# Layer norms of a two-layer perceiver block: GpSimd makes the offset, ScalarE scales the rows, and one norm stands for two

## The reference

```python
def _layernorm(x, axis=-1, eps=1e-05):
    m = jnp.mean(x, axis=axis, keepdims=True)
    v = jnp.var(x, axis=axis, keepdims=True)
    return (x - m) / jnp.sqrt(v + eps)

x = x + cross_attention(ctx, _layernorm(x))        # 16 heads, 4096 keys
x = x + top64_attention(_layernorm(x))             # 16 heads, 256 keys, only the 64 largest scores
x = x + switch_ffn(_layernorm(x))                  # 8 experts, capacity 128
x = x + context_attention(_layernorm(x), ctx)      # 1 head, 4096 keys
x = x + state_space(_layernorm(x))                 # both directions, see below
x = x + tile_ffn(_layernorm(x))                    # 8 tiles, one chosen per row
```

## Time and profile before

| | |
|---|---|
| median of 3 runs | 1524.51 us (1522.3 to 1524.8) |
| the profiled execution | 1535.18 us, its span 1533.7 us |
| PE busy, share of the span | 1304.3 us, 85% |
| PEld | 805.7 us, 53% |
| DVE | 1259.5 us, 82%, 3917 instructions |
| ACT | 973.0 us, 63%, 1505 instructions |
| POOL | 418.7 us, 27%, 316 instructions |
| mean granted PE clock, share of full | 0.909 |

### The profile page before, as it was taken

One profiled execution on the slowest core, in us unless ns is written; L12 is line 12 of the kernel. 1 busy time (PEld: TensorE's weight loads), 2 busy tenths in 40 slices (PEclk: granted clock), 3 DMA queues, 4 the chain that ended last, 5 costly groups with the idle time before them and its releaser, 6 DMA issues. The chain is left out here.

```text
span 1533.7 us, 31701 instructions
## 1 busy us (share of the span) xinstructions
PE 1304.3 (85%) x11784; PEld 805.7 (53%) x11784; DVE 1259.5 (82%) x3917; ACT 973.0 (63%) x1505; POOL 418.7 (27%) x316
## 2 busy tenths in 40 slices
PE   7999899998999988999958597678879789567746
PEld 4555566655665655666634484366347446323313
DVE  1355059999999998999999999998997787878983
ACT  6777778888786876878833353266677578434330
POOL 4110012232322213222222321222343343422450
PEclk9999999999998998999979799879979979678767
DMA  7878320333213320330005122104466356223320
GB/s 158 216 189 266 57 32 30 53 57 57 29 29 57 57 32 28 57 53 14 33 23 176 42 78 89 55 29 136 137 170 180 102 139 180 79 59 111 93 74 7
DMA packets 96856, 132.69 MB, mean 87 GB/s; under 512 B 20192, under 2 KB 80872, under 8 KB 93744
## 3 DMA queue, kind: packets, MB, share of 16 engines
q1 hardware_dynamic: 96688, 130.50, 33.6%
HBM read 124.95 MB, written 5.51 MB: 85 GB/s over the span
## 5 line engine op out<-in xcount | busy, mean ns | idle before, releaser
L1434 ACT ACTIVATE attn_arena<-ps 128x1024 f32<-128x1024 f32 x512 | 497.5, 1025 | 142.4 <-PE ps L456 139.6
L2066 DVE MATCH_REPLACE8 attn_late<-attn_shared,attn_late 128x256 f32<-128x256 f32 x1024 | 411.6, 410 | 0.0
L2063 DVE MAX8 attn_shared<-attn_late 128x8 f32<-128x256 f32 x1024 | 381.3, 415 | 11.9 <-ACT attn_late L1460 10.7
L456 PE MATMUL ps<-attn_arena 32*128 32x256 f32 x4096 | 343.0, 407 | 7.8 <-ACT attn_arena L1434 3.2
L470 PE MATMUL ps<-attn_arena 128*32 128x256 f32 x4096 | 279.0, 389 | 6.5 <-ACT attn_early L1442 3.0
L456 PEld LDWEIGHTS ps<-attn_arena 32*128 32x128 f32 x4096 | 231.4, 188 | 92.8 <-issue 65.4
L1297 POOL TENSOR_SCALAR attn_late<-attn_late 128x512 f32<-128x512 f32 x64 | 95.7, 1495 | 595.1 <-DVE attn_late L2066 595.1
L470 PEld LDWEIGHTS ps<-attn_arena 128*32 128x32 f32 x4096 | 109.2, 110 | 138.8 <-issue 63.1
L739 PE MATMUL ps<-attn_arena,attn_q 128*128 128x512 f32 x256 | 134.4, 660 | 15.0 <-DMA attn_arena<-ctxT 15.0
L1310 POOL TENSOR_TENSOR attn_late<-attn_late 128x1024 f32<-128x1024 f32 x48 | 113.2, 2362 | 121.5 <-DVE ps L1889 121.5
L761 PE MATMUL ps<-attn_arena 128*128 128x256 f32 x512 | 128.1, 396 | 0.0
(11 more groups left out here) (249 smaller groups left out, 1622.7 us busy)
## 6 DMA issues: line engine op xcount, KB each, us to landing
attn_arena<-ctxT SPq DMA_DIRECT2D x124, 256.0 KB, 4.7
attn_arena<-ctx SPq DMA_DIRECT2D x32, 512.0 KB, 4.2
attn_late<-rows SPq DMA_DIRECT2D x256, 64.0 KB, 2.3
attn_arena<-ctxV SPq DMA_DIRECT2D x15, 1024.0 KB, 13.0
attn_late<-maskT SPq DMA_DIRECT2D x20, 512.0 KB, 6.6
attn_late<-wide SPq DMA_DIRECT2D x64, 128.0 KB, 2.7
attn_early<-wide SPq DMA_DIRECT2D x64, 128.0 KB, 3.3
attn_arena<-maskT SPq DMA_DIRECT2D x12, 512.0 KB, 11.9
```

Source lines behind the costliest of these rows:

```text
L456: mm = pe.matmul(ps[:, first + j - 2 * i, u * S:(u + 1) * S], kx[n % 2][rows, k0:k0 + P], qpad[rows, n % GROUPS, b * S:(b + 1) * S], start ...
L1434: act.activation(probs[m % 2][:, 2 * i:2 * i + 2], ps[:, first:first + 2, :], ACT.Exp, scale=1.0 / 16.0).then_inc(exp_done, 1)
L2063: dve.max(top[:, t, turn], s[:, i, t] if turn == 0 else work[:, i, t]).then_inc(picked, 1)
L2066: dve.match_replace(work[:, i, t], top[:, t, turn], s[:, i, t] if turn == 0 else work[:, i, t], LOW).then_inc(picked, 1)
```

## The change

For the norms `out`, `place` and `fx` DVE stops after `ve`; POOL makes `rstd` and the offset -mean * rstd (`nmean`), and ACT writes the rows as Identity(x * rstd + nmean) in a slot of its own. For the state space block one set of statistics is left. With v the first variance, the second norm has factor rstd * spread, with spread = (v * rstd^2 + EPS)^-0.5, and the residual x + n has factor rstd + 1; POOL works both out in ten small instructions and ACT writes `xs` and `X` from them. `x0` and `xn` stay as they were. POOL waits for `normed` (ACT done with the last factors) before it writes `rstd` again; DVE waits for the last `rstd_ready` before it writes new statistics.

```diff
+def norm_order():
+    first = {("x0", b): FIRST_P + (b + 1) * 2 for b in range(B)}
+    first |= {("xn", b): H * b - LEAD + 2 for b in range(B)}
+    first |= {(name, b): DUE[name][b][0] + 1 for name in ("out", "place") for b in range(B)}
+    first |= {("ssm", b): SSM_P[b] - 6 for b in range(B)}
+    first |= {("fx", b): FFN_P[b] + 9 for b in range(B)}
+    return {name: i for i, name in enumerate(sorted(first, key=first.get))}
...
-            def root(k):
+            def root(k, alone=False):
                 pool.wait_ge(var_ready, k + 1)
-                pool.tensor_tensor(rstd[:], ve[:], mhalf[:], ALU.pow).then_inc(rstd_ready, 1)
+                pool.wait_ge(normed, scaled[0])
+                power = pool.tensor_tensor(rstd[:], ve[:], mhalf[:], ALU.pow)
+                if alone:
+                    power.then_inc(rstd_ready, 1)
+                    return
+                scaled[0] += 1
+                step(power)
+                step(pool.tensor_tensor(nmean[:], mv[:, :, 0], rstd[:], ALU.mult))
+                pool.tensor_scalar(nmean[:], nmean[:], -1.0, None, ALU.mult).then_inc(rstd_ready, 1)
+
+            def roots_twice(k):
+                pool.wait_ge(var_ready, k + 1)
+                pool.wait_ge(normed, scaled[0])
+                scaled[0] += 1
+                step(pool.tensor_tensor(rstd[:], ve[:], mhalf[:], ALU.pow))
+                step(pool.tensor_tensor(spread[:], rstd[:], rstd[:], ALU.mult))
+                step(pool.tensor_tensor(spread[:], spread[:], mv[:, :, 1], ALU.mult))
+                step(pool.tensor_scalar(spread[:], spread[:], EPS, None, ALU.add))
+                step(pool.tensor_tensor(spread[:], spread[:], mhalf[:], ALU.pow))
+                step(pool.tensor_tensor(twice[:], rstd[:], spread[:], ALU.mult))
+                step(pool.tensor_tensor(nmean[:], mv[:, :, 0], rstd[:], ALU.mult))
+                step(pool.tensor_scalar(nmean[:], nmean[:], -1.0, None, ALU.mult))
+                step(pool.tensor_tensor(ntwice[:], nmean[:], spread[:], ALU.mult))
+                pool.tensor_scalar(rstd[:], rstd[:], 1.0, None, ALU.add).then_inc(rstd_ready, 1)
...
                 for b in batches(-6, p):
-                    root(roots[0])
-                    root(roots[0] + 1)
-                    roots[0] += 2
-                    pool.wait_ge(xs_ready, b + 1)
+                    roots_twice(roots[0])
+                    roots[0] += 1
+                    pool.wait_ge(xs_ready, T * (b + 1))
...
+            def scale_rows(name, b, rows, ready):
+                act.wait_ge(rstd_ready, norm_index[name, b] + 1)
+                act.activation(rows[:, 0], X[:, b * T], ACT.Identity, scale=rstd[:, 0:1], bias=nmean[:, 0:1]).then_inc(ready, 1)
+                act.activation(rows[:, 1], X[:, b * T + 1], ACT.Identity, scale=rstd[:, 1:2], bias=nmean[:, 1:2]).then_inc(ready, 1)
+                act.wait_ge(ready, T * (b + 1))
+                act.sem_inc(normed, 1)
+
+            def scale_twice(b):
+                name = "ssm"
+                act.wait_ge(rstd_ready, norm_index[name, b] + 1)
+                for t in range(T):
+                    act.activation(xs[:, t], X[:, b * T + t], ACT.Identity, scale=twice[:, t:t + 1], bias=ntwice[:, t:t + 1]).then_inc(xs_ready, 1)
+                for t in range(T):
+                    x = X[:, b * T + t]
+                    act.activation(x, x, ACT.Identity, scale=rstd[:, t:t + 1], bias=nmean[:, t:t + 1]).then_inc(x_summed, 1)
+                act.wait_ge(x_summed, T * (b + 1))
+                act.sem_inc(normed, 1)
...
             def late_duties(p, slot):
...
+                for b in due_after("out", p - 1):
+                    if b < B - 1 and slot == 0:
+                        scale_rows("out", b, xm, xm_ready)
+                for b in due_after("out", p):
+                    if b == B - 1 and slot == 1:
+                        scale_rows("out", b, xm, xm_ready)
+                for b in due_after("place", p):
+                    if slot == (3 if b == B - 1 else 2):
+                        scale_rows("place", b, xc, xc_ready)
+                if slot == 2:
+                    for b in batches(-6, p):
+                        scale_twice(b)
+                if slot == 0:
+                    for b in ffn_batches(10, p):
+                        scale_rows("fx", b, xm, fx_ready)
...
-            def normalise(k, x, out):
+            def normalise(k, x, out=None):
+                if k > B:
+                    dve.wait_ge(rstd_ready, k)
                 for t in range(T):
                     step(dve.bn_stats(stats[:, t], x[:, t]))
                     step(dve.bn_aggr(mv[:, t], stats[:, t]))
                 dve.tensor_scalar(ve[:], mv[:, :, 1], EPS, None, ALU.add).then_inc(var_ready, 1)
+                if out is None:
+                    return
...
             def ssm_norms(b):
-                x = X[:, b * T:(b + 1) * T]
-                step(normalise(norms[0], x, xs))
-                norms[0] += 1
-                dve.tensor_tensor(x, x, xs, ALU.add).then_inc(dve_step, 1)
-                count[0] += 1
-                normalise(norms[0], xs, xs).then_inc(xs_ready, 1)
+                normalise(norms[0], X[:, b * T:(b + 1) * T])
                 norms[0] += 1
...
                     for b in batches(9, p):
+                        dve.wait_ge(x_summed, T * (b + 1))
                         add(b, "sout")
```

More of the change, by code:

```diff
@@ L289, in attention @@
         ve = sb("ve", [P, T])
-        rstd = sb("rstd", [P, T])
+        rstd, nmean = sb("rstd", [P, T]), sb("nmean", [P, T])
+        twice, ntwice, spread = sb("twice", [P, T]), sb("ntwice", [P, T]), sb("spread", [P, T])
         mhalf = sb("mhalf", [P, T])
@@ L399, in attention @@
         ssm_loaded, a_exp, a_ready, ssm_zeroed, ssm_consts = sem("ssm_loaded"), sem("a_exp"), sem("a_ready"), sem("ssm_zeroed"), sem("ssm_consts")
-        xs_ready, xs2_ready, cv_ready, u_ready, xcd_ready = sem("xs_ready"), sem("xs2_ready"), sem("cv_ready"), sem("u_ready"), sem("xcd_ready")
+        xs_ready, x_summed, xs2_ready, cv_ready, u_ready, xcd_ready = sem("xs_ready"), sem("x_summed"), sem("xs2_ready"), sem("cv_ready"), sem("u_ready"), sem("xcd_ready")
         rows_stored, bc_loaded, act_step, l_ready, dt_ready = sem("rows_stored"), [sem(f"bc_loaded{i}") for i in range(BC_HELD)], sem("act_step"), sem("l_ready"), sem("dt_ready")
@@ L420, in attention @@
         PICKS = 4 * (TOPK // 8)
-        misc, branch = {}, {}
+        misc, branch, norm_index = {}, {}, norm_order()
         block = ctx.enter_context(nc.Block())
@@ L957, in _ @@
                     for b in due("xm", p, slot):
-                        pe.wait_ge(xm_ready, b + 1)
+                        pe.wait_ge(xm_ready, T * (b + 1))
                         turn_rows("xm", b, xm)
@@ L966, in _ @@
                     for b in due("xc", p, slot):
-                        pe.wait_ge(xc_ready, b + 1)
+                        pe.wait_ge(xc_ready, T * (b + 1))
                         turn_rows("xc", b, xc)
@@ L1318, in _ @@
             pool.memset(kx[0][:, FIRST_KT * P:], 0.0).then_inc(kx_zeroed, 1)
-            root(0)
+            root(0, alone=True)
             pool.wait_ge(x0_ready, 1)
@@ L1346, in _ @@
                 if p - FIRST_P + 1 in INTRO:
-                    root(INTRO[p - FIRST_P + 1])
+                    root(INTRO[p - FIRST_P + 1], alone=True)
                 if 0 <= p - 1 < B * H:
@@ L1364, in _ @@
                 if ending and d == 2:
-                    root(roots[0])
+                    root(roots[0], alone=True)
                     roots[0] += 1
@@ L1967, in between @@
                         add(b, "out")
-                        normalise(norms[0], X[:, b * T:(b + 1) * T], xm).then_inc(xm_ready, 1)
+                        normalise(norms[0], X[:, b * T:(b + 1) * T])
                         norms[0] += 1
@@ L1977, in between @@
                             add_expert(b)
-                            normalise(norms[0], X[:, b * T:(b + 1) * T], xc).then_inc(xc_ready, 1)
+                            normalise(norms[0], X[:, b * T:(b + 1) * T])
                             norms[0] += 1
@@ L2034, in between @@
                     for b in batches(9, p):
+                        dve.wait_ge(x_summed, T * (b + 1))
                         add(b, "sout")
                     for b in ffn_batches(9, p):
-                        normalise(norms[0], X[:, b * T:(b + 1) * T], xm).then_inc(fx_ready, 1)
+                        normalise(norms[0], X[:, b * T:(b + 1) * T])
                         norms[0] += 1
```

6 lines of the change are left out of this document (3 added, 3 removed).

## The result

Five runs of the changed kernel took 1507.67 to 1515.83 us, median 1512.98, against 1524.8 us for the kernel before (1522.3 to 1526.79): ratio 0.9914 (95% interval 0.9889 to 0.994). A second set gave 1511.88 us and 0.9900 (0.9879 to 0.9922). The change saves 12 to 15 us; 17.3 were forecast.

The account below looks back on a forecast made before the run. DVE was taken to bound the attention steps, with mixed bounds in the scan steps. The terms -15.3 + 1.6 + 2.8 + 1.7 - 5.4 - 3.3 + 0.6 sum to -17.3 us: 1507.2 us from 1524.5, range 1488 to 1516.

Parts of the forecast that it names:

- rival 2: Attention steps: PE takes part of the gain, about 5 to 10 us lost, 1512 to 1517 us; chance 0.14 together with rival 4.
- Steps 20 to 58: Six plain norms and one state space norm relieve DVE and PE can follow: -15.3 us, ends 0 and -17.
- 3 (all): Slots where ACT waits for POOL: PE and ACT's stream becomes the bound, +16.8 us, 1541 us; chance 0.05.
- Steps 66 to 73: Forecast for steps 66 to 72: DVE's relief absorbed, POOL's L1310 starts later behind ACT: +1.6 us, ends -8.7 and +3.
- step 74: Same chain through POOL, SP's keys and PE; L1310 later, delay comes through at once: +2.8 us, ends -5.4 and +5.
- Steps 81 to 83: fx of batch 0 delays make_log, +1.7 us; batch 3's state space norm gets its rows sooner, -5.4 us.
- the row that it had allowed to shrink: DVE's 3.38 us row at 1340.03, beside POOL's L1310; shrinking by 2.35 us would make step 83's gain -7.8 us.
- The rest: fx of batches 1 and 2, in steps where DVE runs through with short waits: -3.3 us, end 0.
- The tail: Last fx, serial: DVE's 0.82 us become 0.55 us on POOL and 0.91 us on ACT: +0.6 us.
- Relief in full: Whole kernel: all of DVE's norm relief counts, 39.3 us, giving 1485.2 us; chance 0.23 for it or most of it.
- rival 4: New ACT lines: Identity loads a function table each time, about 1517 us; chance 0.14 together with rival 2.

Follow-up runs that it names:

- before_weigh: Kernel before, with POOL's first weigh_states of state space norm steps moved right behind the two roots, ahead of the norm_w and norm_b products; ratio 1.0011.
- ssm_only: Changed kernel with norms out, place and fx back on DVE, so only the state space norm is changed; ratio 0.9970 to the kernel before.
- after_keys: Changed kernel with SP's context key loads one slot earlier, ahead of the B and C loads; ratio 0.9883 to the kernel before.
- after_store: Changed kernel with SP's stores of dt and du ahead of the first B and C load of their step; ratio 0.9924 to the kernel before.
- after_both: Changed kernel with both SP moves, key loads one slot earlier and stores ahead of the first B and C load; ratio 0.9861 to the kernel before.
- after_fx: Changed kernel with ACT writing the fx rows at the end of slot 1, behind make_log, instead of in slot 0; ratio 0.9890 to the kernel before.
- plain_only: Changed kernel with the state space block's two norms back on DVE, so only out, place and fx are changed; ratio 0.9971 to the kernel before.
- before_both: Kernel before with both SP moves, key loads one slot earlier and stores ahead of the first B and C load; ratio 0.9983.
- before_keys: Kernel before with SP's context key loads one slot earlier, ahead of the B and C loads; ratio 1.0008.
- after_weigh: Changed kernel with POOL's first weigh_states of state space norm steps ahead of its wait for ACT's rows and the norm products; ratio 0.9857 to the kernel before.
- after_all: Changed kernel with all four moves: SP's keys and stores, POOL's weigh_states, ACT's fx rows; 1499.89 us, ratio 0.9824 to the kernel before.

## Why the prediction was right, and where not

From the median of 1524.5 us the forecast was 1507.2 us, with 1500 to 1511 as its own range. Measured are 1512.98 and 1511.88 us, 1 to 2 us outside that range and inside the wide one (1488 to 1516). By the number alone rival 2 (1512 to 1517) fits about as well; what decides is where the time went, stretch by stretch. There the terms miss by 0.2 to 1.9 us, with both signs, so that the sum (-15.0 against -17.3) is no further off is in part luck.

**Steps 20 to 58: -15.3 forecast, -13.4 measured.** The mechanism is as written. Step 58 after the change:

```profile
966.15 0.17 DVE L1805 TENSOR_SCALAR attn_ve<-attn_mv 128x2 f32<-128x2 f32 x1
966.23 1.21 DVE L1895 TENSOR_REDUCE attn_mx<-attn_arena 128x1 f32<-128x1024 f32 x1
```

DVE goes on at once, where 5.44 us lay before. Each plain norm moved the following selects by 1.7 us against before_weigh (1.65 forecast), and step 58 by 4.2 to 4.8, by the profile compared (5.44; 5.5 in ssm_only). Between steps 46 and 54 up to 0.9 us are given back; what takes them is not shown. Less than 2 of the 15.3 us are missing. So PE's room was enough for nearly all of it, and rivals 2 (5 to 10 us lost) and 3 (all) are out.

**Steps 66 to 73: +1.6 forecast, -0.2 measured; step 74: +2.8 forecast, +2.1 measured.** That the 5.44 us of two norms would be absorbed, and that step 74 would even lose, was the step that made the forecast, and it held: at scans 4 and 5 the profile after had gained 5.7 us more than at scan 0 (-26.2 us against -20.5), and at scan 10 it was back at -20.7; at step 74, from scan 20 to 24, it went from -26.4 to -18.0. At step 66 the delay was smaller than forecast: L1344 starts 9.4 us after `ve` began, 9.2 before. Step 74 after the change, in order:

```profile
1187.40 0.17 DVE L1805 TENSOR_SCALAR attn_ve<-attn_mv 128x2 f32<-128x2 f32 x1
1188.61 1.22 DVE L1953 TENSOR_TENSOR ps<-attn_late,attn_early 128x1024 f32<-128x1024 f32 x1
1188.71 1.17 POOL L1201 TENSOR_TENSOR attn_spread<-attn_spread,attn_mv 128x2 f32<-128x2 f32 x1
...
1192.21 0.22 POOL L1208 TENSOR_SCALAR attn_rstd<-attn_rstd 128x2 f32<-128x2 f32 x1
1194.79 1.09 ACT L1643 ACTIVATE attn_early<-X,attn_ntwice,attn_twice 128x256 f32<-128x256 f32 x2
1195.97 1.27 POOL L1436 TENSOR_TENSOR attn_early<-attn_early,attn_arena 128x512 f32<-128x512 f32 x1 [3.54 <-ACT attn_early L1643]
1198.87 2.79 POOL L1344 TENSOR_TENSOR attn_late<-attn_late 128x1024 f32<-128x1024 f32 x1
1201.68 1.71 SPq L1112 DMA_DIRECT2D attn_late<-rows  x4
1203.44 1.85 SPq L1092 DMA_DIRECT2D attn_arena<-ctxT  x4
...
1207.22 0.43 SPq L1116 DMA_DIRECT2D wide<-attn_early  x1
...
1207.57 5.70 PE L749 MATMUL ps<-attn_arena,attn_q 128*128 128x512 f32 x8 [4.77 <-DMA attn_arena<-ctxT]
...
1213.39 1.86 SPq L1132 DMA_DIRECT2D attn_early<-wide  x4
...
1216.84 1.22 DVE L1895 TENSOR_REDUCE attn_mx<-attn_arena 128x1 f32<-128x1024 f32 x1 [6.11 <-ACT attn_arena L1563]
...
1218.22 1.23 DVE L1953 TENSOR_TENSOR ps<-attn_late,attn_early 128x1024 f32<-128x1024 f32 x1 [0.16 <-DMA attn_early<-wide]
```

POOL has its ten small ones done at 1192.43, stands 3.54 us for ACT, which is in `make_log` until 1194.4, and starts L1344 11.5 us after `ve` began (9.2 us before). Everything behind it on SP starts from there. What the forecast got wrong is what hangs on it. It named the keys alone, and said that PE's wait for them would grow; it is 4.77 us here and 4.95 at step 66, not longer than the 5.11 and 5.00 of the earlier trace rows. The wait that grew is DVE's, 6.11 us now at L1895 and 1.21 us at the same place before:

```profile
1234.87 1.22 DVE L1826 TENSOR_REDUCE attn_mx<-attn_arena 128x1 f32<-128x1024 f32 x1 [1.21 <-ACT attn_arena L1530]
```

after_keys and after_store, each without effect, and after_both with 6 to 8 us show that the stores are a second chain of the same length; they stand in the kernel before too, and the forecast left them out.

**Steps 81 to 83: +1.7 and -5.4 forecast, -3.7 together; -2.2 measured.** The stretch from scan 30 to 44 shows -3.9, but 1.7 of that is `fx` of batch 1, which lies between scans 43 and 44. The remaining -2.2 us hide two larger errors that partly cancel: `fx` of batch 0 cost 4.7 us instead of 1.7, and the state space norm gave 6.7 instead of 5.4; the last 0.2 us are in a wait for PE. That the sum is near is luck. Step 82:

```profile
1292.23 1.24 POOL L1193 TENSOR_SCALAR attn_nmean<-attn_nmean 128x2 f32<-128x2 f32 x1
...
1293.50 0.60 ACT L1634 ACTIVATE attn_xm<-X,attn_nmean,attn_rstd 128x256 f32<-128x256 f32 x1 [7.05 <-POOL attn_nmean L1193]
...
1296.32 0.45 ACT L1599 ACTIVATE attn_early<-ps,attn_arena 128x256 f32<-128x256 f32 x1
...
1308.28 0.69 DVE L1848 TENSOR_TENSOR X<-X,ps 128x512 f32<-128x512 f32 x1 [6.37 <-PE ps L736]
```

and the same place in after_fx:

```profile
1291.45 0.47 ACT L1599 ACTIVATE attn_early<-ps,attn_arena 128x256 f32<-128x256 f32 x1 [2.63 <-PE ps L808]
...
1295.51 0.58 ACT L1634 ACTIVATE attn_xm<-X,attn_nmean,attn_rstd 128x256 f32<-128x256 f32 x1
...
1304.26 0.69 DVE L1847 TENSOR_TENSOR X<-X,ps 128x512 f32<-128x512 f32 x1 [3.60 <-PE ps L736]
```

`make_log` began 0.7 us after `ve` before and begins 5.4 us after it now, so 4.7 us late, not 1.7: behind the rows stood the decays of slot 0 as well (1.70 us at 1294.71), one POOL instruction took 1.24 instead of 0.22 us, and the pair of ACT 1.09 us instead of 0.91. That comes through in full: scan 38 of plain_only, counted from scan 0, is 4.7 us later than in the kernel before, with this norm's own relief of DVE already in it. after_fx takes 3.7 us of it back.

The state space norm of step 83, alone in ssm_only, gives 7.9 us. 5.5 of them are there by scan 38, DVE's relief as forecast. Another 1.2 us are a DVE instruction that ran beside POOL's L1310 before and does not now; before, then after:

```profile
1334.38 1.40 DVE L1920 CAST attn_idxf<-attn_idx 128x2 f32<-128x2 uint32 x1
...
1315.04 0.17 DVE L1984 CAST attn_idxf<-attn_idx 128x2 f32<-128x2 uint32 x1
```

The forecast had no such term; the row that it had allowed to shrink, 3.38 us, still takes 3.40 us (L1953 beside POOL's L1344). The last 1.2 us are a shorter wait of DVE for PE behind scan 40, which before_both shows too, without any change of the norms.

**The rest.** `fx` of batches 1 and 2: -3.3 forecast, -3.1 measured, 1.7 us between scans 43 and 44 and 1.4 from there to scan 63. The tail: +0.6 forecast, +1.8 measured for the whole stretch behind the last scan. From the end of `ve` to PE's first matmul it is 2.54 us now, 1.71 before (the earlier trace rows begins this path), so 0.83 us is the norm's. The other 1.0 us is probably the clock's: behind the last scan the kernel before is at the lower level for 24 us and the one after for 32, and before_both, whose norms are unchanged, has 32 us there as well and a tail 0.8 us longer than before. The three profiles with 24 us have tails of 44.3 or 44.4 us, all others 45.1 or more. Why the level lasts longer is not shown.

```profile
1478.16 0.17 DVE L1805 TENSOR_SCALAR attn_ve<-attn_mv 128x2 f32<-128x2 f32 x1
...
1479.73 0.60 ACT L1634 ACTIVATE attn_xm<-X,attn_nmean,attn_rstd 128x256 f32<-128x256 f32 x1 [21.23 <-POOL attn_nmean L1193]
...
1480.87 1.11 PE L692 MATMUL ps<-ident,attn_xm 128*128 128x128 f32 x4 [4.91 <-ACT attn_xm L1635]
```

**Rivals.** Relief in full (39.3 us) is out, for the reason forecast. No function table is loaded at the new lines (37 loads before and after); rival 4 is out.

## What to carry to other kernels

Before work moves to another engine's queue, list what stands behind it there, and what stands behind the engine that will wait for it; the gain of 5.44 us at a norm became nothing because one multiplication on GpSimd, on which two DMA chains hang, was behind a wait for ScalarE. When a relief is absorbed, look for more than one chain: moving either of two equal ones shows nothing, moving both, or their common head, shows it. A reordering that is worthless before a change can be worth half of the change's gain after it.

## What the runs showed of the hardware

- A POOL instruction on 128x2 elements (the power apart) takes 0.19 to 0.24 us, but in four cases 1.16 to 1.24 us; each of these starts 0.05 to 0.11 us after DVE's 1.22 us L1953 (1188.71 and 1292.23 above). The prediction counted only what POOL does to DVE. The Trainium skill, "SBUF — State Buffer", section "Who interferes with whom", has one lock for the shared port pair, so it acts both ways; the trace agrees with that. These four make up some 3.9 of POOL's 8.6 us beyond the forecast; its 62 `weigh_states`, 2.43 us on the mean instead of 2.36, are some 4.2 us of it. DVE is held as well: the CAST of step 83 takes 1.39 or 1.40 us in before, before_keys, before_both and plain_only, and 0.17 us in after; in after_weigh and after_all an instruction just behind it takes 2.19 instead of 0.23 us. So a shift of a microsecond moves such a cost, or removes it.
- ACT's Identity with a factor and an offset per row from SBUF takes 1.09 us for two 128x256 tiles, against 0.91 us for the exponentials of L1474 that stood for it: 0.09 us more for each.
- The granted clock is part of the result. The profile before spent 280 us at 1.2 GHz, the one after 252, after_weigh 228: here the programs that wait less spent less time at the lower level, though after_all, faster still, spent 248 there, and before_weigh (270) and before_keys (260), equally fast, show how far it varies by itself. One wait of DVE for PE (1.66 us near 484 us, behind a stretch of 10.2 us at the lower level that began at 472) is in the profile of before, and with 1.55 and 1.63 us in those of before_keys and before_both, behind the same 10.2 us; before_weigh, with 3.4 us at the lower level there, and after, with none, do not have it.
